# Attention pieces in halves over two quarters, and q and k of a unit earlier, in a transformer with a routed feed-forward on one core

## The reference

```python
# layer 1: plain attention, then a layer norm
q, k, v = heads(x @ Wq.T + bq), heads(x @ Wk.T + bk), heads(x @ Wv.T + bv)
attn = softmax(q @ k.T / sqrt(16)) * head_mask
x = layernorm(x + (attn @ v) @ Wo.T + bo)
# layer 2: causal attention with rope, then a mixture of experts
n = rmsnorm(x, g1)
q, k, v = rope(heads(n @ wq)), rope(heads(n @ wk)), heads(n @ wv)
h = x + (softmax(causal(q @ k.T / 4)) @ v) @ wo
n = rmsnorm(h, g2)                       # 8 experts, the best 2 of each token
y = h + sum_of_top2(p_e * ((silu(n @ wg[e]) * (n @ wu[e])) @ wd[e]))
out = layernorm(x + y)
```

## Time and profile before

| | us |
|---|---|
| median of 3 runs | 1440.64 |
| lowest and highest | 1439.84, 1443.2 |
| the profiled execution | 1439.77 |
| its span | 1438.0 |
| busy over the span: PE, DVE, ACT, POOL | 1271.7, 956.0, 827.7, 797.1 |
| attention, both layers | about 890 |
| the chain that ended last, PE L1650 and L1672 | 19% and 11% of the span |

### The profile page before, as it was taken

The page is one execution under the profiler, slowest core; times in us unless marked ns, Lnnn a source line. Parts: engine busy times, 40 slices in busy tenths (PEclk is TensorE's granted clock), DMA queues, the critical chain, the costliest instruction groups (busy, mean ns, idle before and its releaser), DMA issues. The chain is left out here.

```text
span 1438.0 us, 33091 instructions
## 1 busy us (share of the span) xinstructions
PE 1271.7 (88%) x11455; PEld 705.8 (49%) x11456; DVE 956.0 (66%) x1760; ACT 827.7 (58%) x1673; POOL 797.1 (55%) x835
## 2 busy tenths in 40 slices
PE   4999999999989999899999963399999999999990
PEld 1222322223223443344444432378888888888880
DVE  7888888988897888887898613734444444444443
ACT  4178788888878767566667741134434433444334
POOL 5144557547456665856554234056666666666644
PEclk9799999999999999999999975599999999999995
DMA  6345767767687787868675434693322222322326
GB/s 186 69 97 166 174 181 205 202 192 201 180 212 202 224 234 205 228 203 220 175 178 165 120 99 145 182 275 52 46 43 44 47 46 43 47 43 44 44 31 241
DMA packets 159005, 204.46 MB, mean 142 GB/s; under 512 B 31217, under 2 KB 121329, under 8 KB 158897
## 3 DMA queue, kind: packets, MB, share of 16 engines
q1 hardware_dynamic: 141424, 182.55, 46.3%
q0 software_dynamic: 17472, 20.50, 9.1%
HBM read 111.46 MB, written 82.87 MB: 135 GB/s over the span
## 5 line engine op out<-in xcount | busy, mean ns | idle before, releaser
L978 ACT ACTIVATE a_probs<-a_ps_s 128x512 f32<-128x512 f32 (+2 forms) x896 | 459.9, 569 | 156.1 <-PE a_ps_s L746 150.9
L1053 DVE TENSOR_REDUCE a_shift_max<-a_ps_m 128x1 f16<-128x512 f32 x512 | 320.4, 682 | 50.1 <-PE a_ps_m L751 48.8
L751 PE MATMUL a_ps_m<-a_qkx 48*128 48x128 f16 (+3 forms) x1408 | 284.1, 301 | 19.7 <-DVE a_shift_max L1053 9.7
L1650 PE MATMUL e_ps_gu<-e_xT,w_up 128*128 128x256 f16 x2574 | 297.2, 274 | 2.6 <-ACT e_xT L1704 2.6
L746 PE MATMUL a_ps_s<-a_qkx 49*128 49x128 f16 (+3 forms) x1408 | 276.1, 296 | 15.1 <-ACT a_probs L978 15.1
L1650 PEld LDWEIGHTS e_ps_gu<-e_xT,w_up 128*128 x2574 | 249.4, 98 | 35.5 <-issue 6.5
L847 PE MATMUL a_ps_o<-a_probs,a_v_one 128*32 128x512 f32 (+3 forms) x2048 | 234.2, 530 | 2.7 <-ACT a_o L985 2.6
L746 PEld LDWEIGHTS a_ps_s<-a_qkx 49*128 49x128 f16 x1408 | 90.0, 95 | 267.3 <-ACT a_probs L978 155.7
L1586 POOL DMA_INDIRECT h<-e_y,e_put x78 | 125.1, 1604 | 88.8 <-DVE e_y L1746 57.6
L448 POOL TENSOR_TENSOR a_o_half<-a_o_half,a_inv_half 128x512 f32<-128x512 f32 x32 | 40.6, 1269 | 227.3 <-DMA a_inv_half<-a_inv_dram 221.9
L1672 PE MATMUL e_ps_y<-w_down,e_h 128*128 x1326 | 154.1, 273 | 9.3 <-issue 6.7
(11 more groups left out here) (194 smaller groups left out, 1664.4 us busy)
## 6 DMA issues: line engine op xcount, KB each, us to landing
a_qkx<-a_qk_dram SPq DMA_DIRECT2D x192, 128.0 KB, 4.3
a_qk_dram<-a_qk SPq DMA_DIRECT2D x32, 512.0 KB
a_o_dram<-a_o SPq DMA_DIRECT2D x64, 256.0 KB, 2.6
a_o_half<-a_o_dram SPq DMA_DIRECT2D x32, 256.0 KB
a_inv_half<-a_inv_dram SPq DMA_DIRECT2D x32, 256.0 KB
part<-a_part SPq DMA_DIRECT2D x16, 512.0 KB, 5.8
a_q_swap<-a_q SPq DMA_DIRECT2D x64, 128.0 KB
spare<-in_wg SPq DMA_DIRECT2D x16, 352.0 KB, 5.6
```

The costliest lines, as they stand in the source:

```text
L751: return pe.matmul(out, qx[first:first + 48, r, pair, q * P:(q + 1) * P], kx[first:first + 48, r, pair, k0:k1], start=start, stop=stop)
L978: act.activation(dst, src, ACT.Exp).then_inc(exp_out, 1)
L1053: vector.tensor_reduce(out, src, AX.X, ALU.max, negate=True).then_inc(max_out, 1)
L1650: mm = pe.matmul(ps_gu[:, bank, kind, f % 2], w[:, ds(e, 1)].rearrange("p o f -> p (o f)"), xT[:, s, xh, k, :], start=n == 0, stop=n == 5)
```

## The change

The table is rewritten. A heavy piece that stands at i = 2 is made in halves in quarters 1 and 2 of its step, one at i = 3 in quarter 3 and in quarter 0 of the next step (half_piece). The four qk pieces of unit u + 2 now stand at g = 0, 0, 1, 2 where they stood at g = 1, 1, 3, 3; v for unit u + 1 at g = 1 and for unit u + 2 at g = 3; out at the end of g = 2 and in g = 3. A light piece stands at the end of quarter 0 or 2, behind weigh (light_piece), and is emptied at the start of the next quarter, ahead of that quarter's tiles (empty_light). The residual of out moves from g = 2 to g = 3. turn is for unit u + 3 and stands in g = 2 and 3. POOL splits a half at even n in both layers and turns it at odd n; DVE does rope_cos at odd n, rope_sum at even n. SP swaps and loads q and k at odd n, ahead of load_rows, and stores them at even n, ahead of load_o. split_x and load_x move too. No arithmetic is added or taken away.

```diff
         u, g = n // G, n % G
         kind, v, k = {
-            (0, 0): ("turn", u + 2, 0), (0, 1): ("turn", u + 2, 1), (0, 2): ("v", u + 1, 0), (0, 3): ("v", u + 1, 1),
-            (1, 0): ("parts", u - 3, 1), (1, 1): ("rows", u, 1), (1, 2): ("qk", u + 2, 0), (1, 3): ("qk", u + 2, 1),
-            (2, 0): ("logits", u - 3, 0), (2, 2): ("out", u - 1, 0), (2, 3): ("out", u - 1, 1),
-            (3, 0): ("parts", u - 2, 0), (3, 1): ("rows", u + 1, 0), (3, 2): ("qk", u + 2, 2),
-            (3, 3): ("qk", u + 2, 3)}.get((g, i), (None, 0, 0))
+            (0, 0): ("parts", u - 3, 0), (0, 2): ("qk", u + 2, 0), (0, 3): ("qk", u + 2, 1),
+            (1, 0): ("rows", u, 1), (1, 1): ("parts", u - 3, 1), (1, 2): ("v", u + 1, 1), (1, 3): ("qk", u + 2, 2),
+            (2, 0): ("logits", u - 3, 0), (2, 1): ("turn", u + 3, 0), (2, 2): ("qk", u + 2, 3), (2, 3): ("out", u - 1, 0),
+            (3, 0): ("rows", u + 1, 0), (3, 1): ("turn", u + 3, 1), (3, 2): ("out", u - 1, 1),
+            (3, 3): ("v", u + 2, 0)}.get((g, i), (None, 0, 0))
...
-        for i in range(4):
+        for i in (0, 2, 1, 3):
...
                 if n % 2 == 0:
-                    swap((n + 6) // 2)
-                    load_qk((n + 4) // 2)
                     if g == 0:
                         store_part(u - 3)
                         load_res(u - 1)
-                    elif u + 3 > 0:
-                        load_x(u + 3)
+                        if u + 3 > 0:
+                            load_x(u + 3)
                     store_o(n - 1)
                     for m in weights_at(n - 1):
                         store_weights(m)
                         load_weights(m + 2)
+                    store_qk((n + 6) // 2)
                     load_o(n // 2 - 1)
                 else:
+                    swap((n + 7) // 2)
+                    load_qk((n + 5) // 2)
                     load_rows((n + 1) // 2)
...
-                    store_qk((n + 5) // 2)
...
-                    h = (n + 6) // 2
-                    if plain(h // 2):
-                        split_high(h)
-                        split_low(h)
                     if g == 0:
                         factors(u - 2)
-                        split_x(u + 2)
                     else:
                         part_low(u - 2)
-                    turn_half(h)
+                    split_high((n + 6) // 2)
+                    split_low((n + 6) // 2)
+                    if g == 2:
+                        split_x(u + 3)
+                    for m in weights_at(n):
+                        split_weights(m)
                 else:
-                    h = (n + 5) // 2
-                    if causal(h // 2):
-                        split_high(h)
-                        split_low(h)
+                    turn_half((n + 7) // 2)
                     if g == 1:
                         bias(u - 1)
+                    for m in weights_at(n):
+                        split_weights(m)
                     normalise((n - 3) // 2)
                     if g == 3:
                         add_residual(u - 1)
-                for m in weights_at(n):
-                    split_weights(m)
...
+            def half_piece(n, quarter):
+
+                j = (quarter + 1) % 2
+                piece = piece_at(n - 1, 3) if quarter == 0 else piece_at(n, 3 if quarter == 3 else 2)
                 if piece is None:
                     return
                 kind, u, k = piece
-                if numbers[piece] > 0:
-                    pe.wait_ge(piece_out, numbers[piece])
+                if j == 0:
+                    free_piece(piece)
                 if kind == "qk":
-                    project(u, k)
+                    project(u, k, j)
                 elif kind == "v":
-                    project_v(u, k)
-                elif kind == "turn":
+                    project_v(u, k, j)
+                else:
+                    project_out(u, k, j)
+            def light_piece(n, quarter):
+
+                piece = None if quarter % 2 else piece_at(n, quarter // 2)
+                if piece is None:
+                    return
+                kind, u, k = piece
+                free_piece(piece)
...
-                    a_piece(n, quarter)
+                    half_piece(n, quarter)
...
+                    light_piece(n, quarter)
...
-                    act.wait_ge(pv_mm, 16 * (u - 1))
+                    act.wait_ge(pv_mm, 16 * (u - 1) - (2 if i == 0 else 0))
...
-            def empty_piece(n, i):
-                piece = piece_at(n, i)
+            def empty_piece(n, quarter):
+                piece = piece_at(n, 2) if quarter == 2 else piece_at(n - 1, 3) if quarter == 0 else None
...
+            def empty_light(n, quarter):
+                piece = piece_at(n, quarter // 2) if quarter % 2 else None
...
-                    early = (1 if quarter < 2 else 0) if causal(u) else 3
+                    early = 0 if causal(u) and quarter >= 2 else 1
+                    empty_light(n, quarter)
...
+                if n % G == 3 and quarter % 2 == 0:
+                    residual(n // G - 1, quarter // 2)
+
+            def empty_light(n, quarter):
                 u, g = n // G, n % G
-                if g == 0 and quarter == 1:
-                    move_x(u + 2)
-                elif g == 1 and quarter == 0:
+                if g == 1 and quarter == 3:
                     move_parts(u - 3)
-                elif g == 2 and quarter == 0:
+                elif g == 2 and quarter == 1:
                     move_logits(u - 3)
-                elif g == 2 and quarter >= 2:
-                    residual(u - 1, quarter - 2)
+                elif g == 3 and quarter == 3:
+                    move_x(u + 3)
...
-                        if i == (0 if early else 3):
+                        if i == 1:
...
-                            rope_cos((n + 6) // 2, quarter)
+                            rope_sum((n + 6) // 2, quarter)
                         elif quarter == 3:
                             join_maxima((n + 2) // 2)
                     else:
-                        if quarter < 2:
-                            rope_sum((n + 5) // 2, quarter)
                         if quarter == 1:
                             invert((n - 3) // 2)
+                        if quarter in (1, 2):
+                            rope_cos((n + 7) // 2, quarter - 1)
```

90 lines of the change are left out of this document (49 added, 41 removed).

## The result

The changed kernel takes 1540.66 us (median of 4 runs, 1535.04 to 1541.52) where the kernel before took 1441.92 in the same comparison: a ratio of 1.067, 95% interval 1.063 to 1.071. It is slower by about 99 us, far outside the range of 1425 to 1463. The profiled execution took 1535.04 us, its span 1533.0.

The account below looks back on a forecast made before the run. Three engines were taken to share the bound in the plain layer, PE almost alone in the causal one. Terms -5.5 + 2 - 2.5 + 13, queues at 0, gave +7 us: 1447 us from 1439.8, range 1425 to 1463.

Parts of the forecast that it names:

- Queues: SP's transfers ahead of the rows and POOL's wait for the swap at odd steps: 0 (0 to +5) us.
- The bank: Causal layer: PE waits for the single bank behind light pieces, 5.4 us each in units 11 and 12, 27 in all.
- The causal layer's sum: Bank waits and change-overs of 31 us, less 10 won and 8 overlapping: +13 us (-2 to +25).
- Units 5 to 7: Rope and turns join in, with more DVE work in g = 3: +2 us (-3 to +6).
- the 10 us that it took as won: Causal layer: waits of a residual for part_low and first maxima for load_qk, moved a step apart, save 10 us.
- Plain layer and start: Halved pieces starve ACT and DVE less: units 0 to 4 -5.5 us (-12 to -1), start -2.5 (-6 to +4).
- Plain layer wins: Rival: plain units gain 2.4 us each, causal layer loses only 2; 1425 us, expected 1424 to 1437; chance 0.30.
- the collisions of DVE and POOL: Rival: rope_sum collides with POOL's work, about 1463 us; sign is a mean rope_sum above 1.5 us; chance 0.10.
- What would show it: Signs: plain unit 49.5 us, unit 12 51 us, 1 us waits for a_xT and a_nT, no residual wait for part_low.

Follow-up runs that it names:

- e14: The change with rows, inv and load of o first, POOL's turn behind normalise, DVE's sums two quarters later, store of q and k at odd steps: 1458.8 us, 1.010.
- e5: The change's pieces, halves and light pieces, with the q and k chain on SP, POOL and DVE back in its old steps: 1465.8 us, ratio 1.020.
- e15: e14 with the heavy pieces whole again from unit 7 on: 1440.4 us, ratio 0.999.
- e10: e5 with the heavy pieces whole again from unit 7 on: 1455.2 us, ratio 1.007.
- e4: The change with 20 pairs of extra PE products ahead of the wait for the rows, in step g = 2 of causal units: 1532.6 us, ratio 1.063.
- e11: Changed schedule through unit 4 with rows, inv and load of o first and POOL's turn behind normalise, then the schedule of before: 1433.4 us, ratio 0.993.
- e3: The change with the rows' two loads issued from ScalarE's queue instead of SP's: 1525.2 us, ratio 1.058.

## Why the prediction was wrong, step by step

**The step that failed is "Queues", the term taken at 0 (0 to +5).** It measured some 82 us: 1540.7 with the change's order, 1458.8 (e14) with the same pieces and swap, turn, split and load as early, but in an order in which no urgent work waits behind them. Against the old queues (e5) it is 68 by the ratios. The text had named what matters (four swaps and six loads ahead of the rows; POOL's wait at the start of odd steps) and priced each alone. Three things were wrong.

1. *The deadline.* "the rows wait until the next step, and a step is 11.5 us" counted a whole step of slack. The rows leave SP 5.4 us of issuing later and are there 8.6 us after that; PE ran out at 572.6, before they were even issued. The price per time, 1.1 us, was taken from a wait for another transfer; in units 9 to 13 it was 10.0, 5.3, 8.1, 4.7 and 3.5.
2. *Busy time as room.* POOL's 26.73 us of 46.2 busy was read as room. But its wait for the swap came to 100.4 us of 300, and a wait at the head of an in-order engine delays all that stands behind it, and on POOL that was the normalisation and the next split.
3. *The loop.* The chain was not followed once round: SP's swap, POOL's turn, DVE's sum, POOL's split, SP's store, and again SP's swap. Before, each link had its place behind the step's urgent work, and the round fitted into two steps (22 to 27 us). In the change it takes 26 to 32, in the round shown 29.6. A delay on it is not paid once; it comes back every two steps.

How the 82 us split among the links can't be said as a sum, since each edit alone moved the wait elsewhere: rows first gave 34, the rows on another queue 15, load_o first nothing, and the turn last on top of rows first took 133. Of the kernels that keep the chain sooner in the causal layer, only e14 and e15 came near the kernel before. They have rows, inv and the load of o first, turn and sums late and the store of q and k a step later; which of these could be left out is open.

**The bank** was right in mechanism and nearly in size. The forecast had 5.4 us of waits in a full unit; unit 12 of e5 shows 5.2 (2.3, 0.9, 0.7, 0.2, 0.6, 0.6). The forecast's 31 us of waits and change-overs, less the 8 that overlap with waits of before, are 23, and whole pieces gave back 17 to 18 (e5 to e10, e14 to e15).

**The causal layer's sum** came out short all the same. It had +13 for units 8 to 13; in e14, without the loss on the queues, they take 24.5 us more than before (312.9 and 288.4), just inside the range. Units 5 to 7 take 7 us more, where the forecast had 2. What failed in it is the 10 us that it took as won: of the two kinds of wait named there, DVE's for part_low is gone in e14 and one of 2.1 us is left for load_qk, but in e15, with the bank's waits gone as well, units 8 to 13 are still 8.5 us longer than before and not shorter. With the queues at 0, as assumed, the time would have been inside the range: e14 is 15 us above before by its ratio, where the text had 7.

A cost that the bank's sum did not have is what follows a wait, PE's clock. Unit 12 of e5, two stretches of it around the 2.3 us wait:

```profile
706.00:710.00 4.00, 1.70 (x19) 0.78 (x15) 3.65 (x5) 0.38 (x1) 2.36 (x2) 1.00 0.41 122
710.00:718.00 8.00, 8.00 (x75) 2.64 (x74) 3.99 (x7) 3.99 (x7) 3.02 (x3) 0.57 0.96 222
```

PE is busy 1.70 of 4 us and then works for 8 us at a clock of 0.57, mostly the lower of its two levels (0.50 is 1.2 GHz). If all of its work in them goes by the clock, that is an estimated 8 x (1 - 0.57) = 3.4 us more for one wait of 2.3, where PE is the bound. e4 showed that it costs little where PE is not.

**Plain layer and start.** In the change itself units 0 to 4 lost 5.1 us, where the forecast had a gain of 5.5; PE's waits for the rows are 7.4 us there between 90 and 340. With the rows first and inv ahead of the swaps the gain came: in e11 units 0 to 4 take 7.1 us less and the first store of o leaves 0.9 us earlier, 8.0 in all, where the text had 5.5 + 2.5. (At its last store 5.7 are left: units 8 to 13, with the schedule of before, take 4.9 us more.) That the two sums agree is in part luck, since the first store leaves anywhere between 87.5 and 91.6 us in the experiments, whose start hardly differs. In the start itself DVE's first maximum comes at 35.81 us, 0.6 later than before, where the forecast had 4 (0 to 7); in the experiments it comes at 34.7 to 37.5.

```profile
35.81 1.29 DVE L1077 TENSOR_REDUCE a_shift_max<-a_ps_m 128x1 f16<-128x512 f32 x2 [0.51 <-PE a_ps_m L767]
```

**Rivals.** "Plain layer wins" is true of the plain layer alone, and not in the change but in e11. The sign set for the collisions of DVE and POOL did not come: the mean of the 32 rope sums is 0.95 us (before: 0.75), not over 1.5. They did get somewhat longer: the median is 0.68 as before, but 14 of them take more than 0.8 us, where 2 did. "What would show it" held for plain unit 3 (49.9), not for units 2 and 4; it held for the waits for a_xT and a_nT, and for the residual's wait for part_low, which is gone. For unit 12 (62.7 instead of 51) it did not.

**What stays open.** e15 has the change's idea without the long loop and without the bank's longest waits, and is 0.999 of before (0.996 to 1.001), though its units 0 to 4 take 7.7 us less. Units 8 to 13 still take 8.5 us more and units 5 to 7 take 5.0 more; PE waits 8.1 us for DVE's maxima there between 500 and 800. Which of the moved works on DVE does that was not tried.

## What to carry to other kernels

When a piece of work is moved to an earlier place on an in-order queue, list what stands behind that place and when each of these is due, and do not go by how busy the engine is. Then follow the moved chain once round all queues until it meets itself: if the round is longer than the steps it has, it becomes the bound, and single edits only push the wait to the next engine. Move the parts of such a chain together, each behind the urgent work of its step, and put engines without room (here DVE) last to wait.

## What the hardware showed

- Behind ten transfers of 128 KB on SP's queue, PE got the two 4 KB loads of the rows 8.6 us after the last was issued, and the 16 KB store of inv landed 8.7 us after its issue began; the median of that store was 6.2 us in the stretch, and 1.4 in the kernel before, which issues swaps and loads in the other step. Put on ScalarE's queue (e3), the rows caused 0.2 us of waits. The Trainium skill (DMA: Bandwidth & Descriptors, section "Two DMAs through the same engine are not ordered") says that within one queue of a DMA engine descriptors start in order; this trace agrees, with the six loads of q and k and then inv landing in the order of their issue, from 575.0 to 582.7 us. In "Queues, rings and completion order" the Trainium skill says that an engine takes turns between its queues. No run here shows that by itself, since in e3 the rows were also issued sooner.
- The granted clock was 0.50, the lower level, from 582 to 587 us behind the wait of 10 us, and 0.57 on the mean over 8 us behind one of 2.3 us. With extra products in the wait for the rows (e4) it was 1.00 over the unit.

```profile
572.00:582.00 10.00, 0.59 (x8) 0.00 (x0) 0.87 (x2) 0.77 (x2) 3.98 (x4) 0.74 0.81 114
582.00:587.00 5.00, 4.42 (x29) 1.42 (x29) 1.53 (x3) 2.46 (x6) 0.74 (x1) 0.50 0.52 152
```
